# Row sums of coefficients through DRAM instead of TensorE, units in natural order, W2 loaded first, the last graph's roots on ScalarE and VectorE

## What is computed

```python
# layer 0: pairwise. hi, hj: 128 x 128, h: 128 x 128 x 128
h = relu(hi[:, None, :] + hj[None, :, :] + b1)       # hi = x @ W1[:128], hj = x @ W1[128:]
y = layernorm(h @ W2 + b2) * gamma + beta
out_i = sum_j adj[i, j] * y[i, j]
# layer 1: graph convolution with D^-1/2 adj D^-1/2, then relu(h @ W.T + b)
# layer 2: (1 + eps) * x + adj.T @ x, then a two-layer perceptron
# layer 3: three times h = relu(layernorm(adj @ (h @ W_i) + b_i + h) * gamma_i + beta_i)
```

## Time and profile before

| | us |
|---|---|
| median of 3 runs | 2756.94 (2756.32 to 2757.82) |
| the profiled execution | 2755.1 |
| its span in the trace | 2753.5 |
| mean granted TensorE clock | 0.989 |

### The profile page before, as it was taken

How to read it: one execution, slowest core, us unless ns; L and a number is a source line. 1 busy time by engine, 2 the same in 40 slices (tenths; PEclk the granted TensorE clock), 3 DMA queues, 4 the chain that set the end, 5 groups by cost and what they waited for, 6 DMA issues and landing times.

```text
span 2753.5 us, 60836 instructions
## 1 busy us (share of the span) xinstructions
PE 2690.3 (98%) x10882; PEld 1147.3 (42%) x10882; DVE 2619.0 (95%) x20102; ACT 2567.7 (93%) x6903; POOL 2487.8 (90%) x3498
## 2 busy tenths in 40 slices
PE   8999999999999999999999999999999999999993
PEld 2344444444444444444444444444444444444442
DVE  4999999999999999999999999999999999999997
ACT  7999999999999999999999999999999999999991
POOL 3899999999999999999999999999999999999992
PEclk9999999999999999999999999999999999999995
DMA  3655655655555555556556555555655565565562
GB/s 108 237 196 209 231 206 196 231 219 194 215 231 201 202 226 219 197 215 231 199 200 232 214 194 221 227 199 203 230 213 197 214 236 196 202 234 210 195 228 95
DMA packets 188668, 571.72 MB, mean 208 GB/s; under 512 B 70656, under 2 KB 106368, under 8 KB 139136
## 3 DMA queue, kind: packets, MB, share of 16 engines
q1 hardware_dynamic: 188288, 567.83, 54.5%
HBM read 555.17 MB, written 8.39 MB: 205 GB/s over the span
## 4 chain that ended last, share of the span: by engine, by line
PE 67%; ACT 18%; DVE 8%; issue 6%; POOL 1%; DMA 0%; SPq 0%; ACTq 0%; DVEq 0%; POOLq 0%
PE y_ps L417 47%; PE ss_ps L429 13%; ACT h L556 11%; DVE h L685 5%; ACT sq L566 4%; ACT dev_rows L573 2%; PE prod_bank L479 1%; PE prod_bank L483 1%; PE prod_bank L450 1%; ACT hid L595 1%; PE prod_bank L456 1%; PE prod_bank L457 1%; PE uv_ps L402 1%; PE uv_ps L403 1%; POOL h L924 1%
## 5 line engine op out<-in xcount | busy, mean ns | idle before, releaser
L924 POOL TENSOR_SCALAR h<-vT,uT 128x128 f32<-128x128 f32 x2520 | 2056.7, 831 | 23.7 <-ACT vT L546 23.3
L417 PE MATMUL y_ps<-h,w2c 128*128 128x512 f32 x4096 | 2016.4, 609 | 11.4 <-DVE h L669 1.6
L685 DVE CUSTOM_DVE_ANT_0 h<-h,cb 128x128 f32<-128x128 f32 x8192 | 1983.9, 289 | 10.0 <-DVE gT_keep L749 0.5
L556 ACT ACTIVATE h<-uv_ps,uT 128x128 f32<-128x128 f32 x4848 | 1409.2, 433 | 0.0
L566 ACT ACTIVATE sq<-y_ps,b2c_col 128x1024 f32<-128x1024 f32 x1024 | 1182.5, 1155 | 112.3 <-PE y_ps L417 112.1
L417 PEld LDWEIGHTS y_ps<-h,w2c 128*128 128x128 f32 x4096 | 682.2, 190 | 903.6 <-issue 723.7
L685 DVE DVE_READ_ACCUMULATOR2_ANT gT<- 128x1 f32 x8192 | 636.8, 78 | 0.1
L429 PE MATMUL ss_ps<-sq,sel 128*32 128x512 f32 x4096 | 545.5, 605 | 0.9 <-ACT sq L566 0.9
L915 POOL TENSOR_TENSOR rs<-var_eps,minus_half 128x1 f32<-128x1 f32 x448 | 302.7, 676 | 35.1
L669 DVE TENSOR_SCALAR h<-vT,uT 128x128 f32<-128x128 f32 x757 | 200.9, 294 | 4.7 <-ACT mask_all L611 2.6
L912 POOL TENSOR_TENSOR var_eps<-mv,eps_col 128x1 f32<-128x1 f32 x448 | 96.1, 215 | 117.9 <-DVE mv L712 115.0
(11 more groups left out here) (100 smaller groups left out, 1489.8 us busy)
## 6 DMA issues: line engine op xcount, KB each, us to landing
cb<-c_scratch SPq DMA_DIRECT2D x384, 1024.0 KB, 9.3
cb<-c_scratch SPq DMA_DIRECT2D x256, 512.0 KB, 4.8
adj_c<-in_adj_dram SPq DMA_DIRECT2D x512, 8.0 KB
devs<-dev_rows SPq DMA_DIRECT2D x512, 8.0 KB
x_in<-in_x_dram SPq DMA_DIRECT2D x64, 64.0 KB, 10.8
c_scratch<-c SPq DMA_DIRECT2D x128, 32.0 KB, 1.5
adj_in<-in_adj_dram SPq DMA_DIRECT2D x64, 64.0 KB, 4.4
x_res<-in_x_dram SPq DMA_DIRECT2D x64, 64.0 KB, 5.4
```

Of the source, the lines that this page charges most:

```text
L417: op = pe.matmul(y_ps[:, t % 2, c0:c0 + COLS], w2c[:], h[:, (SLOTS * g + t) % H_RING, c0:c0 + COLS], start=True, stop=True)
L556: op = act.activation(h[:, (SLOTS * g + t) % H_RING, n * P:(n + 1) * P], v, ACT.Relu, bias=uT[:, b, i:i + 1])
L685: op = dve.tensor_tensor_reduce(h[:, (SLOTS * g + t) % H_RING, cols], h[:, (SLOTS * g + t) % H_RING, cols], cb[:, t // 2, c0:c0 + P], 1.0, ...
L924: op = pool.tensor_scalar(h[:, (SLOTS * g + t) % H_RING, n * P:(n + 1) * P], vT[:, b, :], uT[:, b, i:i + 1], 0.0, ALU.add, ALU.max)
```

## The change

It consists of five parts.

1. The sums of c's halves no longer go through TensorE. After each store of c SyncE stores c_row_sum (128 values) in DRAM, and once per graph reads it back in another shape (c_pair, `load_row_sums`); VectorE adds the two columns. The product L450, the copy to rows_sum and the set-up of row_pick go.
2. `unit_of` gives the natural order, and adj_c comes by two DMAs per graph.
3. `ROOTLESS` holds 4 instead of 5, and three places move: l0_sum from (4, 5) to (4, 7), ln0 from (4, 6) to (4, 8), x1_scaled from (5, 6) to (5, 7).
4. At the start W2 is loaded directly behind x_in, then w1a, w1b and b1, each group with a semaphore of its own, and b2 and gamma0 behind them. Each engine waits only for what its next instruction needs. VectorE's part for b2 and gamma0 is issued at slot 5 of graph 0. TensorE's waits for the later set-up stand two slots behind it.
5. For the last graph alone the roots of the norms are taken by ScalarE (Sqrt with EPS as bias) and VectorE (reciprocal) instead of GpSimd.

```diff
-ROOTLESS = (1, 2, 3, 5, 7, 9, 11, 14)
+ROOTLESS = (1, 2, 3, 4, 7, 9, 11, 14)
...
 def unit_of(t, n):
 
-    half, b = t // HALF, 2 * (t % HALF) + n // BLOCK_UNITS
-    return 64 * half + 16 * (b % 4) + 4 * (b // 4) + n % BLOCK_UNITS
+    return DUO_UNITS * t + n
 
 
 AT = {}
...
 for _name, _slot, _fine in [
     ("adj_turn", 0, 0), ("adj_turned", 0, 6), ("row_sum", 0, 2), ("degree", 0, 5), ("has_degree", 1, 5),
-    ("c_sum_mm", 1, 4), ("c_sum", 1, 8), ("x_base", 2, 3),
-    ("g_keep", 3, 4), ("l0_mm", 4, 0), ("l0_sum", 4, 5), ("ln0", 4, 6), ("x1_scaled", 5, 6),
+    ("c_sum", 1, 8), ("x_base", 2, 3),
+    ("g_keep", 3, 4), ("l0_mm", 4, 0), ("l0_sum", 4, 7), ("ln0", 4, 8), ("x1_scaled", 5, 7),
...
             def load_adj_c_rows(a):
-                rows = a.rearrange("(h q p n) (l j) -> h p q (n l) j", h=2, q=4, p=CHUNKS, l=2)
+                rows = a.rearrange("(h i) (l j) -> h (i l) j", h=2, l=2)
                 for half in range(2):
-                    for p in range(CHUNKS):
-                        sp.dma_start(adj_c[32 * p:32 * p + 32, half, :], rows[half, p]).then_inc(adj_c_in, 16)
+                    sp.dma_start(adj_c[:, half, :], rows[half]).then_inc(adj_c_in, 16)
 
             sp.dma_start(x_in[:], x[0]).then_inc(x_in_in, 16)
+            sp.dma_start(w2[:], l0_W2).then_inc(w2_in, 16)
+            first_weights = [(w1a[:], l0_W1[0:P, :]), (w1b[:], l0_W1[P:2 * P, :]), (b1_col[:], col(l0_b1))]
...
+            for dst, src in first_weights:
+                sp.dma_start(dst, src).then_inc(w1_in, 16)
             weights = [
-                (w1a[:], l0_W1[0:P, :]), (w1b[:], l0_W1[P:2 * P, :]), (b1_col[:], col(l0_b1)),
-                (w2[:], l0_W2), (b2_row[:], row(l0_b2)), (b2_col[:], col(l0_b2)), (gamma0[:], row(l0_gamma)),
+                (b2_row[:], row(l0_b2)), (b2_col[:], col(l0_b2)), (gamma0[:], row(l0_gamma)),
             ]
...
                 wait_apart(sp, c_stored[half], 16 * g)
                 sp.dma_start(c_dram[half].rearrange("(b j) -> b j", j=SPAN), c[:, half, :]
                              ).then_inc(c_stored[half], 16)
+                wait_apart(sp, c_pair_in, 16 * g)
+                wait_apart(sp, rows_stored[half], 16 * g)
+                sp.dma_start(rows_dram[half].rearrange("(p o) -> p o", o=1), c_row_sum[:, half:half + 1]
+                             ).then_inc(rows_stored[half], 16)
+
+            def load_row_sums(g, b):
+
+                for half in range(2):
+                    wait_apart(sp, rows_stored[half], 16 * (g + 1))
+                wait_apart(sp, c_sum_set, g - 1)
+                wait_apart(sp, c_pair_in, 16 * g)
+                sp.dma_start(c_pair[:, b, :], rows_dram.rearrange("h (i l) -> (h i) l", l=2)).then_inc(c_pair_in, 16)
 
             def spread_coefficients(g, half):
...
                     straighten_deviations(old, 1)
                     store_coefficients(old, 1)
                     spread_coefficients(old, 1)
+                    load_row_sums(old, 1 - buf)
                     if new is not None:
                         load_adj_c(new)
                     load_tail(old, 1 - buf)
...
             def products(g, t, block_of_duo):
 
                 if block_of_duo == 0:
+                    if g == 0 and t == 0:
+                        pe.wait_ge(w2c_set, 1)
                     if vector_units(g, t) > 0:
                         wait(pe, h_dve, vector_slots(g, t))
                     if vector_units(g, t) < BLOCK_UNITS:
...
                     pe.transpose(turn_ps[b], adj_in[:, b, :], ident[:]).then_inc(adj_turned, 1)
-                if due("c_sum_mm"):
-                    wait(pe, rows_kept, g + 1)
+                if due("l0_mm"):
                     wait(pe, adjT_set, g + 1)
-                    for half in range(2):
-                        op = pe.matmul(c_sum_ps[b], row_pick[:, half, :], rows_sum[:, half:half + 1],
-                                       start=(half == 0), stop=(half == 1))
-                    op.then_inc(c_summed, 1)
-                if due("l0_mm"):
-                    wait(pe, c_sum_set, g + 1)
                     wait(pe, g_kept, g + 1)
                     pe.matmul(out, gT_keep[:, b, :], w2cg[:], start=True, stop=False)
                     pe.matmul(out, adjT[:, b, :], beta0[:], start=False, stop=True).then_inc(l0_made, 1)
...
                 pe.transpose(prod[1][:, 0:G], mask_f[:], ident[0:G, 0:G]).then_inc(mask_turned, 1)
+
+            def later_set_up_done():
+
                 pe.wait_ge(wT_set, 1)
                 pe.wait_ge(mask_set, 1)
                 pe.wait_ge(pick_set, PARTS)
                 pe.wait_ge(bias_set, PARTS)
                 pe.wait_ge(eps_set, 2)
-                pe.wait_ge(row_pick_set, 3)
+                pe.wait_ge(affine_set, 2)
 
             pe.wait_ge(ident_set, 1)
             turn_x(0, 0)
-            pe.wait_ge(weights_in, 16 * WEIGHTS)
-            pe.wait_ge(w2c_set, 1)
-            pe.wait_ge(affine_set, 2)
+            pe.wait_ge(w1_in, 16 * FIRST_WEIGHTS)
             pe.wait_ge(ones_set, 3)
             pe.wait_ge(set_up, 1)
...
             def squares(g, t):
 
+                if g == 0 and t == 0:
+                    act.wait_ge(b2c_set, 1)
...
                 if g is None:
                     return
+                for name in NORMS:
+                    if g == G - 1 and lo <= AT[name] + 2 < hi:
+                        wait(act, mv_set[name], g + 1)
+                        act.activation(var_eps[:, b:b + 1], mv[:, b, 1:2], ACT.Sqrt, bias=EPS).then_inc(eps_added[name], 1)
...
-            act.wait_ge(weights_in, 16 * WEIGHTS)
             keep_xT(0, 0)
-            act.wait_ge(b2c_set, 1)
+            act.wait_ge(w1_in, 16 * FIRST_WEIGHTS)
...
                     dve.bn_aggr(mv[:, b, :], stats[:, b, :]).then_inc(mv_set[name], 1)
+                if g == G - 1 and lo <= at + NORM_AT - 1 < hi:
+                    wait(dve, eps_added[name], g + 1)
+                    dve.reciprocal(rs[:, b:b + 1], var_eps[:, b:b + 1]).then_inc(rs_set[name], 1)
+
             def norm(g, b, name, dst, lo, hi):
 
                 norm_steps(g, b, name, lo, hi)
...
                 if due("c_sum"):
-                    wait(dve, c_summed, g + 1)
-                    dve.tensor_copy(c_sum[:, b:b + 1], c_sum_ps[b]).then_inc(c_sum_set, 1)
+                    wait(dve, c_pair_in, 16 * (g + 1))
+                    dve.tensor_tensor(c_sum[:, b:b + 1], c_pair[:, b, 0:1], c_pair[:, b, 1:2], ALU.add).then_inc(c_sum_set, 1)
...
-            dve.wait_ge(weights_in, 16 * WEIGHTS)
+            dve.wait_ge(w2_in, 16)
             dve.tensor_reduce(w2_mean[:], w2[:], AX.X, ALU.add).then_inc(w2_meaned, 1)
-            dve.tensor_reduce(b2_mean[:], b2_row[:], AX.X, ALU.add).then_inc(b2_meaned, 1)
             dve.wait_ge(w2_meaned, 1)
             dve.tensor_scalar(w2_mean[:], w2_mean[:], 1.0 / P, None, ALU.mult).then_inc(w2_meaned, 1)
-            dve.wait_ge(b2_meaned, 1)
-            dve.tensor_scalar(b2_mean[:], b2_mean[:], 1.0 / P, None, ALU.mult).then_inc(b2_meaned, 1)
             dve.wait_ge(w2_meaned, 2)
             dve.tensor_scalar(w2c[:], w2[:], w2_mean[:], None, ALU.subtract).then_inc(w2c_set, 1)
-            dve.wait_ge(b2_meaned, 2)
-            dve.tensor_scalar(b2c_col[:], b2_col[:], b2_mean[:], float(P) ** -0.5, ALU.subtract, ALU.mult
-                              ).then_inc(b2c_set, 1)
-            dve.wait_ge(w2c_set, 1)
-            dve.tensor_tensor(w2cg[:], w2c[:], gamma0[:], ALU.mult).then_inc(affine_set, 1)
-            dve.scalar_tensor_tensor(out=b2cg[:], in0=b2_row[:], scalar=b2_mean[:], in1=gamma0[:],
-                                     op0=ALU.subtract, op1=ALU.mult).then_inc(affine_set, 1)
+
+            def first_set_up():
+                dve.wait_ge(weights_in, 16 * WEIGHTS)
+                dve.tensor_reduce(b2_mean[:], b2_row[:], AX.X, ALU.add).then_inc(b2_meaned, 1)
+                dve.wait_ge(b2_meaned, 1)
+                dve.tensor_scalar(b2_mean[:], b2_mean[:], 1.0 / P, None, ALU.mult).then_inc(b2_meaned, 1)
+                dve.wait_ge(b2_meaned, 2)
+                dve.tensor_scalar(b2c_col[:], b2_col[:], b2_mean[:], float(P) ** -0.5, ALU.subtract, ALU.mult
+                                  ).then_inc(b2c_set, 1)
+                dve.wait_ge(w2c_set, 1)
+                dve.tensor_tensor(w2cg[:], w2c[:], gamma0[:], ALU.mult).then_inc(affine_set, 1)
+                dve.scalar_tensor_tensor(out=b2cg[:], in0=b2_row[:], scalar=b2_mean[:], in1=gamma0[:],
+                                         op0=ALU.subtract, op1=ALU.mult).then_inc(affine_set, 1)
...
                 for s in range(SLOTS):
                     if is_graph(new, 1) and s == LATER_SET_UP_SLOT - 1:
                         later_set_up()
+                    if is_graph(new, 0) and s == START + 1:
+                        first_set_up()
...
-                        if ct == HALF + 1 and cg is not None and k == FINE - 1:
```

(23 more changed lines are left out.)

12 lines of the change are left out of this document (7 added, 5 removed).

## The result

The changed kernel takes **3347.1 us** (median of 6 runs, 3342.4 to 3348.3) against 2757.2 us before: ratio **1.2137**, 95% interval 1.2121 to 1.2153. I forecast 2758 with a range of 2746 to 2770. The result lies 577 us above the range's end. The profiled execution has a span of 3344.9 us.

What follows compares the result with a forecast made beforehand. TensorE limits before; afterwards a closed VectorE-GpSimd loop at 42.01 us a graph. Terms +9.3 + 0.2 - 0.3 - 4.4 - 0.2 - 3.0 - 0.4 = +1.2 gave 2756.3 us profiled, 2758 median, range 2746 to 2770.

Steps and rivals of the forecast that it cites:

- Part 1, the small stores: SyncE's row-sum stores between store of c and spread: costed at nothing, bounds 0 and 1.5 us delay per spread.
- VectorE's room: Spread delay VectorE can take without waiting: size unknown; it had waited once in sixty graphs, for 0.2 us.
- The ring's wait at ln0: VectorE waiting at layer 0's normalisation for GpSimd's root: 1.15 us a graph, in place of 0.67 at the product.
- Rival D: Small store delays the spread beyond what VectorE can absorb, two waits a graph, 0.3 us each: 2794 us, chance 0.03.
- The last of my own signs of being wrong: In the next profile, VectorE waiting for cb, the spread coefficients, would show the forecast wrong.
- Part 1, TensorE's saving: Removing L450 passes saves 0.43 us and gives back 0.10: 0.33 us a graph, 41.53 instead of 41.86.
- the ring: Closed loop: dis_raw waits for VectorE's degree_floor, units for dis_raw, VectorE for the root; 42.01 us a graph, +9.3 us.
- all its signs: TensorE under 97%, no L753 wait, about 1.15 us wait at normalisation, 14 units before the root, dis_raw every 42.0 us.
- Two more [units]; I take 1.55: GpSimd's two units added between dis_raw and the root of ln0: 1.55 us together, bounds from 1.44 to 0.84 each.
- rival A: Longer wait at ln0, 1.33 us, from units at 0.84 and a root of 0.95: 2769 us, chance 0.20.
- the further 0.4: Last graph's final stretch: VectorE also loses the last wait at L753 and the copy, 0.4 us.
- The wait at the last z: VectorE's last wait at L753 for TensorE's product, in the last graph: claimed to go, within 0.4 us including the copy.

Runs made afterwards that it cites:

- e3: Changed kernel with the 128 row-sum values stored 512 B apart in DRAM instead of 4 B: 2775.8 us.
- f1: e2 with ROOTLESS and the three moved places put back as before the change: 2738.35 us, ratio 0.9933.
- f2: Changed kernel with sums on TensorE and old ROOTLESS and places, leaving parts 2, 4 and 5 alone: 2748.4 us, ratio 0.9972.
- e2: Changed kernel with row sums sent SBUF to SBUF by four small DMAs a graph, nothing stored in DRAM: 2777.3 us, ratio 1.0074.
- h2: e2 with five of the 128 weighted sums of each graph left out on VectorE, from the third graph on: 2752.5 us.
- e1: Changed kernel with part 1 undone, the half sums going through TensorE again, parts 2 to 5 kept: 2775.6 us, ratio 1.0071.

## Why the prediction was wrong, step by step

- **Part 1, the small stores: this step failed**, and it decides the case. I costed a store of 0.5 KB at its issue, 0.3 us, which hides, and put the bound at 1.5 us of delay, "the landing time of the store of c", which is less than VectorE's room. A store of 256 B runs says nothing of a store of 4 B pieces side by side: the delay is 7.0 us for each half graph. Of these VectorE's room takes some 2 and 5.0 remain. The ring's wait at ln0 goes in exchange, so that a graph takes 8.9 us more than in e3 (51.2 against 42.3), 571 us in all. Rival D had the mechanism (the spread held up, two waits a graph, room of unknown size), with 0.3 us a wait where 5.0 were measured, and a chance of 0.03. The last of my own signs of being wrong, that VectorE waits for cb, is the one that the profile shows. The Trainium skill (DMA: Bandwidth & Descriptors, Specifications) warns of read-modify-write below 512 B. The runs agree that a store of 4 B pieces can be dear; no run shows a read-modify-write. They don't agree that it goes by size alone: the same 4 B writes delayed the reads by 1.2 us at 16 B apart and not at all at 64 B.
- **Part 1, TensorE's saving**: 0.34 us where it was removed, forecast 0.33. Not foreseen was that 0.16 of it is given back when the ring is open (f1), 0.05 of that to ScalarE.
- **Part 2**: nothing, as forecast (graphs every 41.86 us in f2, as before).
- **Part 3, the ring**: right in mechanism, and all its signs are in e2's trace. Its size was 42.27 us a graph in place of 42.01. The term that was mis-sized is "Two more [units]; I take 1.55". They ended at +12.50, against the +12.21 that 0.54, 10.12 and 1.55 make, because units 11 and 12 lost the lighter VectorE that they had beside them before, and 13 and 14 were as slow. The root, 0.86 against 0.90, and what follows up to the next dis_raw, 28.91 against 28.90, were right. VectorE came at +12.04, forecast +11.96. The wait of 1.32 us is rival A's 1.33, by which I had 2769; without the dense stores the kernel takes 2776. A's root of 0.95 was not seen, so that its number fits that well is in part luck. The Trainium skill (GPSIMD Engine Reference, Specifications) has GpSimd in contention with VectorE's instructions with two SBUF inputs, and I took from it that the two added units would run free once VectorE stands still. h2 agrees with the page for units 11 and 12, which take 0.71 and 0.73 us without the weighted sums beside them; what I took from it for units 13 and 14 was wrong, they took 0.83 and 0.94.
- **Part 4, the start**: the first product comes at 4.72, 4.66 us earlier; forecast 4.4. b1's landing sets it, as forecast.
- **Part 5, the last roots**: from mv's end to the normalisation about 0.47 us instead of 0.94 (2718.81 to 2719.28), forecast 0.45. In f2 the seven norms save 2.6 us from the last z of layer 0 to the end (28.8 us for 31.4), forecast 3.0 (0.90 less 0.45 is 0.45, not the 0.43 I multiplied; seven times that is 3.2). f2 keeps the copy of rows_sum, so the further 0.4 can't be read from it; in the changed kernel the stretch takes 28.3 us, 3.1 less than before, forecast 3.4. The wait at the last z, which I had going, is 1.38 us in all three. The trace of f2 has two loads of ScalarE's tables, 1.28 us each and both in its first 32 us, as many as before, and none at the roots. f2 as a whole: 8.1 less measured, 7.6 forecast (4.4, 0.2 and 3.0).

Sum with what was measured: 2757, less 8 for the ends, plus 27 for part 3 (e1 less f2), plus 571 for the stores (the changed kernel less e3) gives 3347. The last term is a difference that includes the result, so this checks only that e1 and e3 agree.
